# Layer 0's masks of tiles 4 to 7 one step earlier on DVE, two of them in other slots of the mask buffer

## The reference

```
layer 0:  e     = leaky(einsum('bid,bjd->bij', x * a0, x))      # leaky slope 0.2; codes 2..4 would use a1..a3
          alpha = sigmoid(where(adj == 1, e, -max))
          x     = layernorm(x + einsum('bij,bjd->bid', alpha, x) + bias)
layer 1:  H = x @ W;  s = H @ a[:256];  d = H @ a[256:]
          e = where(adj != 0, exp(-leaky_relu(s_i + d_j, 0.2)), 0)
          x = layernorm(x + elu((e @ H) / rowsum(e)))
```

## Time and profile before

| | us |
|---|---|
| median of 3 runs (lowest, highest) | 1443.07 (1442.54, 1446.59) |
| the profiled execution's own time | 1447.32 |
| its span in the trace | 1445.6 |

### The profile page before, as it was taken

How to read it: one execution, slowest core, us unless ns; L and a number is a source line. 1 busy time by engine, 2 the same in 40 slices (tenths; PEclk the granted TensorE clock), 3 DMA queues, 4 the chain that set the end, 5 groups by cost and what they waited for, 6 DMA issues and landing times.

```text
span 1445.6 us, 29637 instructions
## 1 busy us (share of the span) xinstructions
PE 1346.6 (93%) x8898; PEld 1206.4 (83%) x8898; DVE 1063.0 (74%) x2654; ACT 935.2 (65%) x2197; POOL 854.3 (59%) x1228
## 2 busy tenths in 40 slices
PE   4799999999999999999999999999999999999986
PEld 3688888988889888888988889888988888888875
DVE  3487877777777777877777777787877787777754
ACT  3676757667585666757657685676757657575742
POOL 3464847558384664837557394764838557384732
PEclk9799999999999999999999999999999999999988
DMA  4113031221303213131321303222121322303100
GB/s 105 30 30 74 23 50 60 45 64 29 76 18 51 65 30 75 22 50 54 51 58 32 73 18 51 65 37 68 25 47 54 51 62 33 69 18 51 37 1 31
DMA packets 55185, 68.18 MB, mean 47 GB/s; under 512 B 5488, under 2 KB 38640, under 8 KB 55152
## 3 DMA queue, kind: packets, MB, share of 16 engines
q0 software_dynamic: 18432, 33.56, 14.8%
q1 hardware_dynamic: 36720, 34.22, 7.3%
HBM read 84.55 MB, written 16.78 MB: 70 GB/s over the span
## 4 chain that ended last, share of the span: by engine, by line
PE 52%; POOL 20%; DVE 11%; issue 7%; DMA 5%; ACT 3%; DVEq 1%; POOLq 0%; SPq 0%; ACTq 0%
PE acc_bank L1203 17%; POOL coef_lo L346 9%; PE hh_bank L1182 5%; DMA code_nat<-in_adj 4%; PE acc_bank L1089 4%; PE acc_bank L1090 4%; PE acc_bank L1091 4%; PE lg_bank L1089 4%; PE lg_bank L1091 4%; PE lg_bank L1090 4%; DVE coef L865 3%; POOL rstd L367 3%; PE tr_bank L1124 3%; POOL rstd L357 2%; POOL var_eps L354 2%
## 5 line engine op out<-in xcount | busy, mean ns | idle before, releaser
L1203 PE MATMUL acc_bank<-H,coef 128*128 128x258 f32 x2048 | 472.9, 384 | 8.9 <-ACT reluP L589 8.1
L1203 PEld LDWEIGHTS acc_bank<-H,coef 128*128 128x128 f32 x2048 | 383.6, 191 | 64.5 <-issue 10.6
L346 POOL TENSOR_TENSOR coef_lo<-coef,coef_hi 128x1024 fp32r<-128x1024 f32 x128 | 306.0, 2391 | 75.1 <-ACT coef_hi L538 73.4
L1089 PE MATMUL acc_bank<-h_hi,coef_hi 128*128 128x256 f32 x1024 | 300.2, 293 | 0.0
L1090 PE MATMUL acc_bank<-h_lo,coef_hi 128*128 128x256 f32 x1024 | 289.0, 282 | 0.0
L1091 PE MATMUL acc_bank<-h_hi,coef_lo 128*128 128x256 f32 x1024 | 288.6, 282 | 0.0
L865 DVE SCALAR_TENSOR_TENSOR coef<-G,E_col,codeT 128x256 f32<-128x256 f32 x512 | 229.3, 513 | 43.0 <-PE acc_bank L1203 36.8
L1089 PEld LDWEIGHTS acc_bank<-h_hi,coef_hi 128*128 128x128 f32 x1024 | 197.3, 193 | 1.1 <-issue 0.2
L1090 PEld LDWEIGHTS acc_bank<-h_lo,coef_hi 128*128 128x128 f32 x1024 | 197.6, 193 | 0.0
L1091 PEld LDWEIGHTS acc_bank<-h_hi,coef_lo 128*128 128x128 f32 x1024 | 197.3, 193 | 0.0
L332 POOL DMA_DIRECT2D code_nat<-in_adj x128 | 73.5, 575 | 202.1 <-PE tr_bank L1124 181.5
(11 more groups left out here) (80 smaller groups left out, 2613.3 us busy)
## 6 DMA issues: line engine op xcount, KB each, us to landing
code_nat<-in_adj POOLq DMA_DIRECT2D x128, 256.0 KB, 3.6
x_raw<-in_x SPq DMA_DIRECT2D x16, 1024.0 KB, 5.6
out<-x SPq DMA_DIRECT2D x128, 128.0 KB, 1.7
W_ext<-in_L_gnn_W SPq DMA_DIRECT2D x1, 256.0 KB, 2.8
score<-in_L_gnn_a SPq DMA_DIRECT2D x1, 256.0 KB, 6.0
bias_bc<-in_L_gnn_bias SPq DMA_DIRECT2D x1, 128.0 KB, 3.9
a_col<-in_L_gnn_a SPq DMA_DIRECT2D x4, 1.0 KB, 2.1
```

The source lines that it names most:

```text
L346: nc.gpsimd.tensor_tensor(coef_lo[:, t % 4, :, :], blocks(coef[:, t % 4, :]), f32(coef_hi[:, t % 4, :, :]), ALU.subtract).then_inc(S.lo0, 1)
L1089: nc.tensor.matmul(dst, lhs_hi, rhs_hi, start=first, stop=False)
L1203: ins = nc.tensor.matmul(acc_bank[t % 2][:, 0:HC], coef[:, SLOT1[t], J * P:(J + 1) * P], H[:, J, :], start=J == 0, stop=J == NT - 1)
```

## The change

Layer 0's tiles get slots by a table SLOT0, in which tiles 4 and 5 lie in slots 4 and 5 and tiles 6 and 7 in slots 0 and 1. The masks of tiles 4 to 7 and their mirrors move one step up, to steps 0 to 3. The waits for free slots follow the table. `high0` and `low0` keep their steps. Core of the diff (the second, general version of the kernel, which doesn't run on these inputs, gets the same table):

```diff
     EDGE = NT // 2
+    SLOT0 = [0, 1, 2, 3, 4, 5, 0, 1]
     SLOT1 = [4, 5, 0, 1, 2, 3, 4, 5]
...
-                nc.gpsimd.tensor_tensor(coef_lo[:, t % 4, :, :], blocks(coef[:, t % 4, :]),
+                nc.gpsimd.tensor_tensor(coef_lo[:, t % 4, :, :], blocks(coef[:, SLOT0[t], :]),
...
-                nc.scalar.activation(coef_hi[:, t % 4, :, :], blocks(coef[:, t % 4, :]),
+                nc.scalar.activation(coef_hi[:, t % 4, :, :], blocks(coef[:, SLOT0[t], :]),
...
-                if t >= 4:
-                    dve.wait_ge(F.lo0, NT * b + t - 3)
+                if t >= 6:
+                    dve.wait_ge(F.lo0, NT * b + t - 5)
                 elif prev:
                     dve.wait_ge(F.agg1, NT * b + t - 5)
...
-                if t == 0 and prev:
-                    dve.wait_ge(F.agg1, NT * b)
-                elif 2 <= t < 6:
-                    dve.wait_ge(F.lo0, NT * b + t + 4)
-                elif t == 6:
+                if t < 6:
+                    dve.wait_ge(F.lo0, NT * b + (6, 8, 4)[t // 2])
+                else:
                     dve.wait_ge(F.agg1, NT * b + 2)
...
-                    if 1 <= t < 3:
-                        mask0_below(b, t + 3, prev)
+                    if t < 2:
+                        mask0_below(b, t + 4, prev)
                     if t >= 1:
                         stats0(F, b, t - 1)
 
                     if t >= 1:
                         moments0(F, b, t - 1)
 
-                    if 3 <= t and t + 3 < NT:
-                        mask0_below(b, t + 3, prev)
-                    if 1 <= t and t + 3 < NT:
-                        mask0_rest(b, t + 3)
+                    if 2 <= t and t + 4 < NT:
+                        mask0_below(b, t + 4, prev)
+                    if t + 4 < NT:
+                        mask0_rest(b, t + 4)
...
-                    if 1 <= t and t + 3 < NT:
-                        mirror(b, t + 3)
+                    if t + 4 < NT:
+                        mirror(b, t + 4)
                     aggregate0(F, b, t, prev)
```

More of the change, by code:

```diff
@@ L794, in mask0_below @@
                         nc.vector.scalar_tensor_tensor(
-                            coef[:, t % 4, j0 * P:j1 * P], tr_bank[m % 2][:, 0:(j1 - j0) * P], 1.0,
+                            coef[:, SLOT0[t], j0 * P:j1 * P], tr_bank[m % 2][:, 0:(j1 - j0) * P], 1.0,
                             codeT[:, t, j0 * P:j1 * P], ALU.add, ALU.mult).then_inc(F.mirror_used, 1)
@@ L803, in mask0_rest @@
                         ins = nc.vector.scalar_tensor_tensor(
-                            blocks(coef[:, t % 4, j0 * P:j1 * P]), score[:, 0:j1 - j0, at:at + P], 1.0,
+                            blocks(coef[:, SLOT0[t], j0 * P:j1 * P]), score[:, 0:j1 - j0, at:at + P], 1.0,
                             blocks(codeT[:, t, j0 * P:j1 * P]), ALU.add, ALU.mult)
@@ L1052, in _ @@
                                     dve.wait_ge(GEN.lo0, NT * b + t - 3)
-                            dst = coef[:, t % 4, :] if k == 0 else score[:, 0, 0:N]
+                            dst = coef[:, SLOT0[t], :] if k == 0 else score[:, 0, 0:N]
                             nc.vector.scalar_tensor_tensor(dst, codeT[:, t, :], float(k + 1), score[:, 0, 0:N],
@@ L1057, in _ @@
                             if k:
-                                ins = nc.vector.tensor_tensor(coef[:, t % 4, :], coef[:, t % 4, :],
+                                ins = nc.vector.tensor_tensor(coef[:, SLOT0[t], :], coef[:, SLOT0[t], :],
                                                               score[:, 0, 0:N], ALU.add)
```

## The result

| | before | after |
|---|---|---|
| median, us (4 runs each, side by side) | 1443.76 | 1474.24 |
| lowest, highest | 1442.54, 1446.59 | 1469.32, 1475.44 |
| the profiled execution's own time | 1447.32 | 1473.78 |
| its span | 1445.6 | 1472.1 |
| mean granted clock of TensorE | 0.983 | 0.976 |

After takes 1.0196 times as long as before, 95% interval 1.0172 to 1.0219. By this ratio it is slower by some 28 us; the two medians of four runs are 30.5 us apart, the two profiled executions 26.5. Forecast were 1468, a range of 1452 to 1479, and 1472 for the profiled execution. The median is 6 us above the forecast, the profiled execution 2 us.

The account below looks back on a forecast made before the run. TensorE's own work (busy 93%) plus gaps fed by GpSimd was taken as the bound. 15 graphs x 1.6 = 24 us, +1 for graph 0, gave 1472 for the profiled execution, 1468 by the median; range 1452 to 1479.

Parts of the forecast that it names:

- (a): DVE, step 0: mask(4) ahead of residual0(0) stands until low0(3) is over; residual0(0) starts at 587.6, 2.2 us late.
- rival without a stall: Mask(4) takes its 0.86 us at step 0, residual0(0) 0.65 late; 0.33 us a graph gained, 1438 us; chance 0.07.
- (b): From residual0(0) to low0(4): rstd(0) 2.3 us late, low0(4) at 591.7, transposes of x(0) from 590.40 to 591.2.
- (c): ACT: norm1 of the old graph's last tile ends at 592.4, not 590.06; x1T(0) moves from 590.89 to 592.35.
- (d): Tile 1: residual0(1) waits for norm1, power0(1) stands behind low0(4); TensorE transposes x(1) at 596.5, 2.45 us late.
- more than forecast: Rival: GpSimd's op slips between mask pieces or mask(6) delays var_eps(1); 2.3 to 2.6 us a graph, 1480; chance 0.13.
- (e): Tile 2: x(2) follows x(1) by 5.0 us on DVE and GpSimd; TensorE transposes it at 601.5, 2.0 us late.
- full stall: The forecast case: mask(4) stands until low0(3) ends; 1.3 to 2.0 us a graph, 1463 to 1474; chance 0.62.
- (f): Tile 3, DVE's step 4 without a mask: var_eps and rstd give 0.76 us back; x(3) 1.6 us late at TensorE.
- (g): Behind x(3) TensorE has no gap, so 1.6 us stay in the graph; layer 1's mask waits cost nothing.
- Graph 0: First graph, low0s packed closer and DVE already idle for the first product: +1 us (0 to +2).

Follow-up runs that it names:

- e3_after_short: The changed kernel with low0(3) cut to 128 of its 1024 columns from graph 1 on: 1458.15 us, 1.0086 of before.
- e9_delay: The kernel before with an unused DVE copy out of PSUM of about 2.2 us ahead of residual0(0) in graphs 1 to 15: 1480.32 us, 1.0226 of before.
- e5_filler: The changed kernel with 16 unused identity transposes on TensorE between project(0) and the wait for x(1): 1463.71 us, 1.0111 of before.
- e6_pool_before: The kernel before with GpSimd reordered: power1(7) at the end of layer 1, low0(3) behind power0(0), low0(4) to low0(7) one step later: 1445.60 us, 0.9990 of before.
- e11_after_free: The changed kernel with GpSimd's mended order, no low0 between the old graph's last moments and norm0(0): 1456.15 us, 1.0086 of before.
- e10_pool_free: The kernel before with low0s later on GpSimd, from graph 1 on low0(3) waiting until norm0(0) has run: 1427.68 us, 0.9877 of before.

## Why the prediction came out, point by point

All times are of the graph read before, in before's time.

- **(a)** Right in the time, with a term missing. residual0(0) starts at 597.00 - 9.43 = 587.57, forecast 587.6. e3_after_short and e9_delay show that both halves of the step hold: low0(3) makes the stall, and the lateness makes the loss. DVE stands idle for 0.60 us ahead of mask(4) and the forecast had it start at once; the stall hides this, since the mask ends with low0(3) whenever it started. The rival without a stall was priced at 1438, faster than before; e3_after_short, which is nearly that case, is 12 to 13 us slower than before, and its rows show this term and a clock that fell in 9 graphs.
- **(b)** Right within 0.2 us: low0(4) at 591.48 (591.7), transposes of x(0) at 591.03 (591.2).
- **(c)** Right: TensorE waits 0.63 us for ACT's x1T(0), as ACT comes late from the old graph's norm1.
- **(d)** Right in mechanism, 0.6 us too large. The transposes of x(1) are at 595.91, 1.87 us late, where 2.45 were forecast. Of the 0.6, some 0.2 are (b), whose low0(4) came that much earlier than forecast, and some 0.3 are the stretch from the end of low0(4) to the end of rstd(1), which I had put at 1.43 us and which took 1.09 (603.26 to 604.35). I let mask(6) lengthen var_eps(1); in fact GpSimd's var_eps(1) starts at 603.21, right at the end of low0(4) and just ahead of the pieces of mask(6) at 603.26, and takes 0.19 us. The rival "more than forecast" had it the other way round.
- **(e)** Wrong by a missing term that cancels the error of (d). The transposes of x(2) are at 601.98, 2.51 us late, where 2.0 were forecast. TensorE's own 4.83 us of work, taken over from the earlier trace rows, were 6.07 at a granted clock of 0.72. With the size that (d) had and no fall of the clock, x(2) would follow 5.01 us behind x(1), at 600.92, and x(3) 4.58 us behind that, at 605.5: 1.0 us late, 15 us over 15 graphs, and with the 3 us of graph 0 18. e5_filler, where the clock doesn't fall, has 16. That the two errors nearly cancel is luck: with (d) as measured and no fall of the clock the sum is these 18 us, 1461 us by the median, below the band given to the full stall.
- **(f)** Right: var_eps(3) and rstd(3) are back at 0.19 and 0.55 us, TensorE has no wait there, and x(3) is 606.36 - 604.48 = 1.88 us late (1.6 forecast).
- **(g)** Right: the transposes of x(4) are 610.93 - 609.08 = 1.85 us late, so nothing is swallowed behind x(3). Over graphs 1 to 14 the mean period went from 86.41 to 87.95 us, 1.54 more (1.6 forecast).
- **Graph 0** was put at +1 and is +3.0. The two pieces of mask(4) there take 4.80 us beside two low0s in a row, and norm0(0) stands beside another. The first two rows are its DVE, the last two, in the second fence, its GpSimd:

```profile
64.83 4.80 DVE L804 SCALAR_TENSOR_TENSOR coef<-score,codeT 128x512 f32<-128x512 f32 x2
...
72.76 2.44 DVE L836 TENSOR_SCALAR x<-resid,moments,rstd 128x256 f32<-128x256 f32 x1 [0.46 <-POOL rstd L358]
```

```profile
58.89 10.60 POOL L347 TENSOR_TENSOR coef_lo<-coef,coef_hi 128x1024 fp32r<-128x1024 f32 x4 [12.87 <-ACT coef_hi L539]
...
72.71 2.34 POOL L347 TENSOR_TENSOR coef_lo<-coef,coef_hi 128x1024 fp32r<-128x1024 f32 x1
```

The sum as measured, from the transposes of x(0) of one graph to those of the next: 3.0 in graph 0, 14 x 1.54 = 21.6, and 1.8 in graph 15 and the end, 26.5 us with the rounding, the difference of the two spans and of the two executions' own times; 25 were forecast. So the sign, the place and the stall were right as a mechanism, and the size rests in part on luck: (d) too large, the clock left out in (e).

The fall of the clock was to be seen in the trace of before. There the distance from x(1) to x(2) is 6.25 to 6.33 us in 4 of the 14 looped graphs, and the clock fell there, as in this one (windows of before, ahead of the transposes of x(1) of that graph and from there to those of x(2)):

```profile
503.80:507.50 3.70, 2.01 (x12) 1.32 (x11) 3.10 (x8) 3.15 (x7) 3.40 (x4) 1.00 0.10 35
507.50:513.90 6.40, 6.32 (x36) 6.06 (x37) 5.65 (x13) 5.00 (x15) 5.67 (x5) 0.73 0.00 0
```

It costs little there, because TensorE had been going to wait for x(2) and x(3) anyway: the next distance was 4.38 us in place of 5.01, and from x(0) to x(4) it is 18.8 to 19.0 us with a fall and 18.7 to 18.8 without. In after those waits are nearly gone, and a fall, which lengthens the stretch by some 1.0 us, costs 0.9. It came in 11 of the 14 looped graphs. In graphs 3, 7 and 11 it did not, with much the same busy time ahead; the window of graph 7:

```profile
688.50:693.40 4.90, 1.99 (x12) 1.31 (x11) 3.32 (x8) 4.35 (x12) 4.57 (x7) 1.00 0.08 27
693.40:698.50 5.10, 4.78 (x36) 4.40 (x37) 4.46 (x10) 4.83 (x13) 4.84 (x5) 1.00 0.00 0
```

What tells these graphs from the others stays open. Open too is how the lock is given when both engines wait for it: GpSimd's var_eps(1) got in ahead of mask(6), and in graph 0 the next low0 got in between the pieces of DVE.

## What to carry to other kernels

Idle time of an engine at its program's position is no free place as long as a neighbour can hold it up there: look at what runs on GpSimd in that very stretch before an operation of DVE with wide operands in SBUF is put into it, and look again for the next one that it meets after every move: in e6_pool_before the low0 that was moved met norm0(0), and the gain was gone. A free neighbour is not enough either. In e11_after_free the mask ran unhindered in that place and the kernel still lost 30 us against e10_pool_free, since what stands ahead of residual0(0) makes x(1) late, and the idle time that the mask was meant to fill had been shorter than the mask. If GpSimd's long operations can be made to wait for the short DVE operation that feeds TensorE, that is worth more than an earlier mask (e10_pool_free, -1.2%). And when a wait of TensorE grows, price the work behind it at the lower clock as well, and see whether the waits that used to absorb this are still there.

## What the runs showed of the hardware

- Masks of two wide fp32 operands in SBUF: the two pieces of mask(4) took 0.86 to 0.89 us with no low0 beside them, 1.90 and 2.50 beside a low0 that had already begun, 4.80 beside two; those of mask(6) 1.16 us behind a low0 and 2.09 beside one. The same holds for norm0, a tensor_scalar of 256 columns with one wide operand: 0.41 us alone, 2.38 to 2.44 when it starts just behind a low0. The Trainium skill (SBUF — State Buffer, section "SBUF: two separate sides") has the exclusive lock for two kinds of DVE operations, those with two inputs in SBUF and those in a mode that uses both ports. The traces agree for the masks, which are of the first kind. norm0 stands in the same way; in which mode it ran no trace shows, and I had not looked for it.
- In after, DVE stands idle 0.59 to 0.64 us in graphs 2 to 14 between the moments that end one graph and the first mask of the next. The trace names nothing to wait for, or TensorE's mirror, which where it is named in these graphs had been over for some 0.6 us. In graph 1, the first of the loop, it is 0.30 us, with the mirror over for only 0.15, and in graph 15, which is written out behind the loop, it is 0.17 us ahead of the same instruction:

```profile
1386.24 0.56 DVE L795 SCALAR_TENSOR_TENSOR coef<-tr_bank,codeT 128x384 f32<-128x384 f32 x1 [0.17 <-issue]
```

  So some 0.4 us a graph belong to the turn of the loop, as far as these rows can tell, an estimate; before, norm1's wait of 0.7 us covered it. It was not tried with an unrolled loop.
- A wait of TensorE can be cheaper filled than empty: 1.91 us of transposes that serve nothing made the kernel after 0.8% faster (1.0111 against 1.0196, each to before on its own chip; the intervals touch), and the clock stayed at 1.00 behind them in 14 of 14 looped graphs.
